# A recurrent chain with its router on one core: who halves the state, who selects, when GpSimd mixes, and how the first loads are cut

## What is computed

```python
def cell(h, x):
    gi = x @ W_ih + b_ih
    gh = h @ W_hh + b_hh
    i_r, i_z, i_n = jnp.split(gi, 3, axis=-1)
    h_r, h_z, h_n = jnp.split(gh, 3, axis=-1)
    r = jax.nn.sigmoid(i_r + h_r)
    z = jax.nn.sigmoid(i_z + h_z)
    n = jnp.tanh(i_n + r * h_n)
    h_new = (1.0 - z) * n + z * h
...
probs = softmax(xt @ w_router)                       # 128 experts
topk_p, topk_idx = top_k(probs, 4)
topk_w = topk_p / (sum(topk_p) + EPS)
basis = silu(xt @ w_gate) * (xt @ w_up)              # K = 8 bases of I = 128 columns
mixed = einsum('tek,tki->tei', mix[topk_idx], basis)
out = einsum('teh,te->th', mixed @ w_down, topk_w * expert_scale[topk_idx])
out = out + silu(xt @ shared_w_gate) * (xt @ shared_w_up) @ shared_w_down
return x + out
```

## Time and profile before

| | |
|---|---|
| median of 3 executions | 148.21 us (148.15 to 151.74) |
| the profiled execution, device time | 147.87 us |
| its span, first to last instruction | 146.0 us |
| TensorE matmul, busy | 136.3 us (93%) |
| TensorE weight load, busy | 98.0 us (67%) |
| VectorE, busy | 111.6 us (76%) |
| ScalarE, busy | 68.1 us (47%) |
| GpSimd, busy | 68.9 us (47%) |

### The profile page before, as it was taken

One profiled execution on the slowest core, in us unless ns is written; L12 is line 12 of the kernel. 1 busy time (PEld: TensorE's weight loads), 2 busy tenths in 40 slices (PEclk: granted clock), 3 DMA queues, 4 the chain that ended last, 5 costly groups with the idle time before them and its releaser, 6 DMA issues.

```text
span 146.0 us, 4048 instructions
## 1 busy us (share of the span) xinstructions
PE 136.3 (93%) x1494; PEld 98.0 (67%) x1494; DVE 111.6 (76%) x411; ACT 68.1 (47%) x222; POOL 68.9 (47%) x123
## 2 busy tenths in 40 slices
PE   7997999999679989999999999999999998899981
PEld 5565767766347658766876687668766875597881
DVE  2215588998967997898789878987898789949661
ACT  1204638565557345535553555255526541522830
POOL 2201115667754893466147614751475148566030
PEclk9999999999999999999999999999999999999999
DMA  3898970000000000010001000100010000000102
GB/s 97 270 369 288 343 235 5 7 0 2 0 0 4 0 0 4 4 36 4 0 0 40 0 0 0 43 0 0 7 36 0 4 7 31 0 0 0 36 4 72
DMA packets 5799, 7.12 MB, mean 49 GB/s; under 512 B 916, under 2 KB 4244, under 8 KB 5780
## 3 DMA queue, kind: packets, MB, share of 16 engines
q1 hardware_dynamic: 5472, 6.70, 13.7%
q10 hardware_dynamic: 308, 0.17, 0.4%
HBM read 5.81 MB, written 1.05 MB: 47 GB/s over the span
## 4 chain that ended last, share of the span: by engine, by line
PE 51%; DVE 34%; ACT 7%; issue 3%; POOL 1%; DVEq 0%
PE unit L604 18%; PE gates L595 11%; DVE sc_out L851 7%; PE down L674 6%; ACT sc_add L412 4%; DVE keys L934 4%; PE gates L559 4%; PE turned L744 3%; DVE pre L842 3%; DVE hT L858 3%; DVE m L839 2%; DVE p L899 2%; DVE wlo L871 2%; PE unit L574 2%; ACT trz L405 2%
## 5 line engine op out<-in xcount | busy, mean ns | idle before, releaser
L299 POOL CAST hThi<-hT 128x64 fp32r<-128x64 f32 x32 | 11.1, 347 | 54.5 <-DVE hT L858 54.1
L604 PE MATMUL unit<-whi,hThi 128*128 128x512 f32 x80 | 33.7, 421 | 2.7 <-POOL wlo L334 2.0
L604 PE MATMUL unit<-wlo,hThi 128*128 128x512 f32 x80 | 31.6, 395 | 0.0
L604 PE MATMUL unit<-whi,hTlo 128*128 128x512 f32 x80 | 31.6, 394 | 0.0
L405 ACT ACTIVATE trz<-gates 128x128 f32<-128x128 f32 x32 | 8.9, 277 | 43.8 <-PE gates L595 43.8
L595 PE MATMUL gates<-whh,hT 128*32 128x192 f32 x512 | 27.4, 332 | 1.7 <-DVE hT L858 1.1
L595 PEld LDWEIGHTS gates<-whh,hT 128*32 128x32 f32 x512 | 13.5, 109 | 12.7 <-DVE hT L858 5.6
L851 DVE TENSOR_TENSOR_SCAN sc_out<-sc_mul,sc_add 128x128 f32<-128x128 f32 x32 | 15.3, 479 | 8.0 <-ACT sc_add L412 7.7
L604 PEld LDWEIGHTS unit<-whi,hThi 128*128 128x128 f32 x80 | 15.1, 188 | 8.7 <-issue 3.5
L604 PEld LDWEIGHTS unit<-whi,hTlo 128*128 128x128 f32 x80 | 15.0, 188 | 3.5
L412 ACT ACTIVATE sc_add<-pre 128x64 f32<-128x64 f32 x32 | 10.3, 322 | 14.5 <-DVE pre L842 14.5
(11 more groups left out here) (129 smaller groups left out, 243.3 us busy)
## 6 DMA issues: line engine op xcount, KB each, us to landing
wraw<-in_L_ffn_w_gate_dram SPq DMA_DIRECT2D x2, 512.0 KB, 6.0
wraw<-in_L_ffn_w_up_dram SPq DMA_DIRECT2D x2, 512.0 KB, 7.8
out_dram<-ot SPq DMA_DIRECT2D x8, 128.0 KB, 2.0
xtok<-in_x_dram SPq DMA_DIRECT2D x7, 128.0 KB, 4.1
wih<-in_L_cond_W_ih_dram SPq DMA_DIRECT2D x2, 384.0 KB, 4.3
whh<-in_L_cond_W_hh_dram SPq DMA_DIRECT2D x1, 512.0 KB, 6.5
whh<-in_L_cond_W_hh_dram SPq DMA_DIRECT2D x1, 256.0 KB, 5.8
wraw<-L_ffn_shared_w_gate_dram SPq DMA_DIRECT2D x1, 256.0 KB, 7.5
```

The costliest lines, as they stand in the source:

```text
L299: pool.tensor_copy(hThi[:, c % 3, :, :, k], hT[:, c % 2, :, k, :]).then_inc(hThi_ready, 1)
L604: last = pe.matmul(dst, st[:, p % 3, s, :, :].rearrange("p b t -> p (b t)"), w[:, s, :, cols], start=(s == 0 and n == 0), stop=(s == KB - ...
```

## The change

- **VectorE to ScalarE:** halving the state (`halve`, after `prepare(t)` in ScalarE's queue), copying the logits, `negmax` and `keys`, and `den`. The router's low weights are now added in the same bank columns by matmuls of 128 columns, so a copy replaces the addition.
- **GpSimd:** the mixing of chunk p - 1 goes over four steps: `scale_basis` 0 and 1 as before, `half` one step later, `quarter` and `mixed` two steps later; `lo_down` goes from step 10 to step 12.
- **Units:** TensorE's slots k = 0 to 3 hold 6, 9, 6 and 9 unit matmuls instead of 9, 9, 6 and 6. `turn_hidden(p - 1)` goes from k = 2 to k = 3, between unit matmuls, and `project` from chunk p - 1 in k = 3 to chunk p - 2 in k = 2. The last router runs before the last unit of chunk 6.
- **Weights and x:** all splitting of weights is a step earlier; the first pair of x blocks is turned in step 0; the steps in `EARLY` are others, as many as before.
- **Start:** 10 warming matmuls instead of 16; h0 is loaded by four DMAs of 32 rows.

```diff
@@ -45,16 +45,16 @@
-WARM = 16
+WARM = 10
...
-EARLY = [4, 5, 6, 7, 10, 11, 14, 15, 18, 19, 22, 23, 26, 27, 30, 31]
+EARLY = [4, 5, 6, 7, 9, 10, 13, 14, 17, 18, 21, 22, 25, 26, 29, 30]
...
-TURN_PAIR = {1: 2, 2: 4, 3: 6}
-KEEP_PAIR_SCALAR = {1: 2}
+TURN_PAIR = {0: 2, 2: 4, 3: 6}
+KEEP_PAIR_SCALAR = {0: 2}
...
-HI_AT = [(0, 0), (0, 0), (0, 0), (0, 2), (2, 4), (4, 6), (6, 8), (8, 10)]
-LO_VECTOR_AT = [[], [], [], [], [2], [4], [5], [8]]
-LO_POOL_AT = [[], [], [], [0], [1], [3], [6], [7], [9]]
+HI_AT = [(0, 0), (0, 0), (0, 2), (2, 4), (4, 6), (6, 8), (8, 10)]
+LO_VECTOR_AT = [[], [], [], [2], [4], [5], [8]]
+LO_POOL_AT = [[], [], [0], [1], [3], [6], [7], [9]]
@@ -313,9 +317,11 @@
-            def add_basis(p):
+            def add_half(p):
...
+            def add_rest(p):
@@ -347,7 +353,10 @@
                 if p >= 1 and k == 0:
...
-                    add_basis(p - 1)
+                if p >= 1 and k == 1:
+                    add_half(p - 1)
+                if p >= 1 and k == 2:
+                    add_rest(p - 1)
@@ -356,13 +365,14 @@
-                    if t == TC + SKEW + 4:
+                    if t == TC + SKEW + 6:
...
-            add_basis(LAST - 1)
+            add_half(LAST - 1)
+            add_rest(LAST - 1)
@@ -376,7 +386,8 @@
         def _(act):
...
-            act.dma_start(h0[:, :], cond.rearrange("b (j c) -> j b c", j=NJ)).then_inc(ld_h0, 16)
+            for j in range(NJ):
+                act.dma_start(h0[Q * j:Q * (j + 1), :], cond[:, FJ * j:FJ * (j + 1)]).then_inc(ld_h0, 16)
...
             def keep_bias():
@@ -411,6 +422,11 @@
+            def halve(t):
+                act.wait_ge(h_ready, t + 1)
+                act.activation(natural(hhalf, slice(0, FJ)), by_block(sc_out, 1), ACT.Copy, scale=0.5)\
+                    .then_inc(hhalf_ready, 1)
             def hi_router():
@@ -433,8 +449,23 @@
+            def copy_logits(p):
+                act.wait_ge(logits_ready, p + 1)
+                if p >= 1:
+                    act.wait_ge(topk_step, TOPK_STEPS * p)
+                act.activation(lx[:, 0:E], route[:, LOGITS], ACT.Copy).then_inc(lx_ready, 1)
+            def topk_keys(p):
+                act.wait_ge(max_ready, p + 1)
+                act.activation(negmax[:, :], v8[:, 0:1], ACT.Copy, scale=-1.0).then_inc(keys_ready, 1)
+                act.activation(keys[:, 0:TOPK], v8[:, 0:TOPK], ACT.Copy).then_inc(keys_ready, 1)
+            def topk_den(p):
+                act.wait_ge(topk_step, TOPK_STEPS * p + 2)
+                act.activation(den[:, :], exsum[:, :], ACT.Identity, bias=sum4[:, :], scale=EPS).then_inc(den_ready, 1)
             def softmax_exp(p):
-                act.wait_ge(topk_step, TOPK_STEPS * p + 3)
+                act.wait_ge(keys_ready, 2 * p + 2)
@@ -480,21 +511,28 @@
                 if p < 0:
                     return
                 if k == 0:
+                    copy_logits(p)
                     if p >= 1:
                         tanh_gate(NU * p - 1)
+                    topk_keys(p)
                 elif k == 1:
                     softmax_exp(p)
                     tanh_gate(NU * p)
+                    topk_den(p)
                 elif k == 2:
                     tanh_gate(NU * p + 1)
-                    copy_emT(p)
+                    tanh_gate(NU * p + 2)
+                elif k == 3:
+                    if p == 0:
+                        hi_down()
+                    tanh_gate(NU * p + 3)
                     if p >= 1:
                         hi_turned(p - 1, turned, slice(0, 3), p)
-                elif k == 3:
-                    tanh_gate(NU * p + 2)
-                    tanh_gate(NU * p + 3)
-                    if p == 0:
-                        hi_down()
+
+            def early_slot(f):
+                p, k = f // TC, f % TC
+                if p >= 0 and k == 2:
+                    copy_emT(p)
             keep_bias()
             for c in range(NC):
@@ -502,14 +540,21 @@
+                    early_slot(t - TC - SKEW)
...
+                    if t < T - 1:
+                        halve(t)
...
+                early_slot(f)
...
+            copy_logits(LAST)
...
+            topk_keys(LAST)
...
+            topk_den(LAST)
@@ -613,37 +670,29 @@
-                    pe.matmul(route[:, LOGITS], hThi[:, p % 3, s, :, :].rearrange("p b t -> p (b t)"),
-                              wrouter[:, s, :, :].rearrange("p a e -> p (a e)"),
-                              start=(s == 0), stop=False, skip_group_check=True)
+                    for a in range(2):
+                        pe.matmul(route[:, LOGITS], hThi[:, p % 3, s, :, :].rearrange("p b t -> p (b t)"),
+                                  wrouter[:, s, a, :], start=(s == 0 and a == 0), stop=False, skip_group_check=True)
...
-                    last = pe.matmul(route[:, 0:E], hTlo[:, p % 3, s, :, :].rearrange("p b t -> p (b t)"),
+                    last = pe.matmul(route[:, LOGITS], hTlo[:, p % 3, s, :, :].rearrange("p b t -> p (b t)"),
...
             def unit(n, blocks):
...
-                if p == 0:
-                    for s in blocks:
-                        i = PIECES.index((u, s))
-                        if i in LO_VECTOR:
-                            pe.wait_ge(w_lo, LO_VECTOR.index(i) + 2)
-                        else:
-                            pe.wait_ge(w_lo_pool, LO_POOL.index(i) + 1)
...
-                last = three(unit_bank[n % NB][:, :].rearrange("p (g n) -> p g n", g=2), p,
-                             slice(UW * u, UW * (u + 1)), blocks)
+                last = three(unit_bank[n % NB][:, :].rearrange("p (g n) -> p g n", g=2), p, u, blocks)
...
             def turn_em(p):
-                pe.wait_ge(topk_step, TOPK_STEPS * p + 5)
+                pe.wait_ge(topk_step, TOPK_STEPS * p + 2)
...
             def coefficients(p):
@@ -723,21 +772,23 @@
                     if k == 0:
                         logits(p)
                         unit(NU * p, range(KB))
-                        unit(NU * p + 1, [0])
                     if k == 1:
-                        unit(NU * p + 1, [1])
-                        unit(NU * p + 2, range(KB))
+                        unit(NU * p + 1, range(KB))
+                        unit(NU * p + 2, [0])
                     if k == 2:
                         turn_em(p)
+                        unit(NU * p + 2, [1])
+                        unit(NU * p + 3, [0])
+                        if p >= 2:
+                            project(p - 2)
+                        coefficients(p)
+                    if k == 3:
+                        unit(NU * p + 3, [1])
                         if p >= 1:
                             turn_hidden(p - 1)
-                        unit(NU * p + 3, range(KB))
-                        coefficients(p)
-                    if k == 3:
-                        if p >= 1:
-                            project(p - 1)
+                        if p == LAST - 1:
+                            logits(LAST)
                         unit(NU * p + 4, range(KB))
-
             def keep_warm(count, dst=turned):
                 for _ in range(count):
@@ -772,10 +823,10 @@
-            logits(LAST)
...
+            project(LAST - 2)
@@ -856,7 +907,6 @@
                 if k == 0 and c >= 2:
...
-                dve.tensor_scalar(natural(hhalf, slice(0, FJ)), by_block(sc_out, 1), 0.5, None, ALU.mult).then_inc(hhalf_ready, 1)
             def lo_router():
@@ -919,42 +969,25 @@
-            def copy_logits(p):
-                dve.wait_ge(logits_ready, p + 1)
-                dve.tensor_reduce(lx[:, 0:E], route[:, LOGITS].rearrange("p (a e) -> p e a", a=2), mybir.AxisListType.X,
-                                  ALU.add).then_inc(lx_ready, 1)
             def topk_max(p):
...
-                dve.max(v8[:, :], lx[:, 0:E]).then_inc(topk_step, 1)
-            def topk_keys(p):
-                dve.wait_ge(topk_step, TOPK_STEPS * p + 1)
-                dve.tensor_scalar(negmax[:, :], v8[:, 0:1], -1.0, None, ALU.mult).then_inc(topk_step, 1)
-                dve.tensor_copy(keys[:, 0:TOPK], v8[:, 0:TOPK]).then_inc(topk_step, 1)
+                dve.max(v8[:, :], lx[:, 0:E]).then_inc(max_ready, 1)
             def topk_mark(p):
-                dve.wait_ge(topk_step, TOPK_STEPS * p + 3)
+                dve.wait_ge(keys_ready, 2 * p + 2)
...
             def topk_em(p):
-                dve.wait_ge(topk_step, TOPK_STEPS * p + 4)
+                dve.wait_ge(topk_step, TOPK_STEPS * p + 1)
...
-            def topk_den(p):
-                dve.wait_ge(topk_step, TOPK_STEPS * p + 5)
-                dve.scalar_tensor_tensor(out=den[:, :], in0=exsum[:, :], scalar=EPS, in1=sum4[:, :],
-                                         op0=ALU.mult, op1=ALU.add).then_inc(topk_step, 1)
-            def topk_rec(p):
-                dve.wait_ge(topk_step, TOPK_STEPS * p + 6)
-                dve.reciprocal(rec[:, :], den[:, :]).then_inc(topk_step, 1)
             def scale_coefficients(p):
```

(27 more changed lines are left out.)

25 lines of the change are left out of this document (20 added, 5 removed).

## The result

| | before | changed |
|---|---|---|
| all timed runs, median | 150.08 us (six runs, 148.15 to 151.98) | 152.61 us (six runs, 151.82 to 154.30) |
| ratio of comparable runs, 95% interval | 1 | 1.0289 (1.0260 to 1.0317) |
| the profiled execution | 147.87 us, span 146.0 | 153.46 us, span 151.7 |

The changed kernel is slower by 2.9%, where 149.8 us and no measurable change were forecast.

The account below looks back on a forecast made before the run. The prediction took TensorE's queue to bind most steps and VectorE one per chunk; 0.4 + 0.1 - 1.65 + 1.3 + 0.4 + 1.0 = +1.55 us gave 149.8 us, with a range of 147.7 to 151.6.

Parts of the forecast that it names:

- What bounds the kernel: Recurrent chunk: TensorE's queue binds steps k=0, 2, 3, VectorE k=1 through the `keys` copy; relief at most 0.23 us per chunk.
- Start, +0.4: Up to the first recurrent step: fewer warming matmuls, but TensorE waits for a later second x block; +0.4 us.
- second x block is late: Rival at the start: four issues take 0.69 each, first step 2.0 later instead of 0.4, 151.4 us; 15%.
- Steps 0 to 7, +0.1: First eight steps: x transposes and weight pieces move earlier, slots of steps 3 to 6 get shorter; sum +0.1 us.
- Steps 8 and 9, -1.65: First selection: waits for `wlo` vanish, step 8 takes 3.4 and step 9 3.07, 6.47 instead of 8.12 us.
- Steps 10 to 13, +1.3: `dlo_w` ahead of `quarter` and `mixed` makes TensorE stand 2.5 us in step 13; 16.3 against 14.98 us.
- T + 4.15: When GpSimd's `mixed` is ready, in us counted from T, the new state of step 12.
- Steps 14 to 30, +0.4: Later chunks: 14.52 against 14.45 us, VectorE's 0.23 eaten by the router's matmuls, 0.22; four chunks +0.3, step 30 3.67.
- the tail, +1.0: Step 31 to last unit matmul: one more `project` 1.08, router 0.2, three unit matmuls 0.7, less `keys` copy 0.97.
- rival of free matmuls: Rival in the router: six short matmuls cost no more than four, 8 x 0.22 less, 148.0 us; 17%.
- ScalarE's work at nothing: ScalarE's new small operations in step k=0 stay within the cover of 0.6 and 0.76 us, so cost nothing.
- The sum: Whole kernel: the terms add up to +1.55 us, 149.4 for the profiled execution, 149.8 for the median.

Follow-up runs that it names:

- b_keys_scalar: Kernel before, with `negmax` and `keys` made by ScalarE instead of VectorE; ratio 0.9981 (0.9950 to 1.0011).
- b_adds_cut: Kernel before, with GpSimd's additions `half`, `quarter`, `mixed` cut to 8 columns from the second chunk on; ratio 1.018.
- b_warm10: Kernel before, with 10 warming matmuls instead of 16; 150.53 us median of ten runs.
- b_both: Kernel before, with h0 in four DMAs and 10 warming matmuls; ratio 1.0103, 149.97 us median.
- a_x_ahead: Changed kernel, with the second x block issued ahead of the four DMAs of h0; ratio 1.0280.
- a_lodown_behind: Changed kernel, with `lo_down` behind `mixed` in the slot of step 12; ratio 1.0163, 150.42 us median.
- a_best: Changed kernel, with h0 in one DMA, 16 warming matmuls, `lo_down` behind `mixed`, router matmuls and VectorE's addition as before; ratio 0.9906.
- b_h0_four: Kernel before, with h0 in four DMAs of 32 rows; ratio 1.0222, 151.41 us median.
- a_h0_one: Changed kernel, with h0 loaded by one DMA again; ratio 1.0225 (1.0149 to 1.0300).
- a_warm16: Changed kernel, with 16 warming matmuls again and h0 still in four DMAs; 154.04 us median.
- a_best24: a_best with 24 warming matmuls instead of 16; 147.95 us median of twelve runs, ratio 0.9979.

## Why the prediction was wrong, point by point

- **What bounds the kernel: right about TensorE, wrong about why VectorE is late.** With VectorE relieved, a chunk is TensorE's in all four steps, 14.49 against 14.52 forecast. But the forecast took the `keys` copy's 0.97 for a cost that goes away with the copy. b_keys_scalar and b_adds_cut show it is a stand behind GpSimd. By b_adds_cut, what frees VectorE in step k=1 is GpSimd's additions going to other steps; the copy's move alone gains nothing measurable. What VectorE's other moved operations add was not run by itself.
- **Start, +0.4: the step that failed.** "I take 0.4, nearest the low bound": the four issues took 1.79 us together, 1.1 more than one, and nothing came back. The block, now issued behind both loads of whh (2.56 and 3.20), was there 2.1 later; that queueing behind them makes the other 1.0 is likely, but no run shows it. The rival *second x block is late* had +2.0 and 15%, and it came near the measured 2.27 for another reason than its own: the issues took 0.45 each, not 0.69. What neither had is the clock. "Six warming matmuls fewer let the bias matmuls start some 0.5 earlier" counts only their time; they are also what brings the clock up, and with ten it was late in eight of ten runs of b_warm10, by their times. By b_both the start costs some 1.5 us in timed runs.
- **Steps 0 to 7, +0.1, measured +0.4:** 26.72 to 27.45 in the variants of the changed kernel with the same first eight steps, against 26.96. Most of the difference within them is step 2, in which TensorE stopped for up to 0.7 in the middle of its matmuls; what stopped it is open.
- **Steps 8 and 9, -1.65, measured -1.0.** No wait for `wlo` is left, as forecast. But step 8 took 3.71, not 3.4, and step 9 3.42, not 3.07: VectorE holds both (0.06 from state to `h_part`), with `em` late behind ScalarE's `ex`, 0.54 for `mix` (beside GpSimd's `wlo`), and in step 9 `p`, `q`, `rec`, `coef` and `p` again ahead of the next gate. A floor of TensorE's was taken where the first selection binds. This is read from the trace alone; no variant tests it:

```profile
43.40 0.86 PE L640 MATMUL gates<-whh,hT 128*32 128x192 f32 x16 [0.25 <-DVE hT L909]
...
46.82 0.86 PE L640 MATMUL gates<-whh,hT 128*32 128x192 f32 x16 [0.27 <-DVE hT L909]
```

- **Steps 10 to 13, +1.3: mechanism and size right, one effect missing.** Forecast 16.3, with `mixed` ready at T + 4.15; measured 16.35 in three variants with the same queue and a steady clock, and T + 4.10 in the changed kernel's profile. On top comes the clock that falls behind the stall, 1.5 us in this profile and in that of a_x_ahead. In how many of the six timed runs it fell there is not known. Four have a mean clock of 0.986 or less, but a low clock at the start does that too (0.977 in a_lodown_behind, which has no stall), and two of the four took only 0.8 us more than the two whose mean clock was 0.994 and 1.0. The forecast said that "the whole recurrence stands" and did not ask what TensorE's clock does then.
- **Steps 14 to 30, +0.4, and the tail, +1.0: right in size** (+0.4, +0.8). In the tail this was luck in part: the 0.97 taken off for the copy of `keys` is the same misreading as above. With the copy alone moved (b_keys_scalar) the tail is 17.64, as before (17.62); what went in the changed kernel are three waits of TensorE for VectorE, 0.38, 0.41 and 0.27. The row's 0.11 for a short matmul held: in a_best two fewer gave back 0.21. The Trainium skill's 56 ns (TensorE: Matmul & The Clock Gate, "Wait — 56ns, not 53.3ns?") does not fit this stream, in which each of the two took 0.10, and the rival of free matmuls fell with it.
- **ScalarE's work at nothing: right.** 0.5 us or more remain from the state to the next `h_part` in all four steps of a chunk.
- **The sum.** Between the two profiles the span grew by 5.7 us where 1.55 was forecast. Of the 4.15 that were missing, the start is 1.9, the clock behind the stall 1.5, steps 8 and 9 0.7 and steps 0 to 7 0.3; the tail was 0.2 cheaper than forecast. For the timed runs the sizes are an estimate: start +1.5 (b_both), steps 8 and 9 -1.0, stall +1.4, chunks +0.4, tail +0.8, and +0.8 for what lowered the clock (the median of 152.6 less the 151.8 of the two runs without it), together +3.9 and 152.1 us; the median was 152.6, so 0.5 is not assigned. The range's upper end (151.6) had the late block but no clock.

## What to carry to other kernels

Price a stall or a start of TensorE twice: the idle time itself, and the matmuls at half pace behind it; so look where a moved operation lets TensorE stand, and keep `lo_down`-like work behind what TensorE waits for. A small operation with an absurd duration (four columns in 0.97 us) can be a wait in disguise: see what another engine runs beside it until the same moment, before giving the operation away. Cutting a small load into several is paid by whatever is issued behind it in the same queue (here 1.79 us of issues instead of 0.65).

## What was not expected of the hardware

- The start has more than one outcome with the same program. With 16 warming matmuls the bias matmuls took 1.04 us in one profile and 1.93 in another, and H(0) was 10.07 to 10.51 or 14.0 to 14.4 (12.85 in b_h0_four, where the wait for the block came between). In timed runs 24 warming matmuls gave no late start in 18 runs, 20 gave one in twelve, 16 in a_best three in six, and 10 on the kernel before eight in ten.
- Behind a wait of 2.4 us TensorE's clock fell in two profiles (the changed kernel's and a_x_ahead's, both at 61.5 us, 0.1 and 1.0 after the wait had ended) and stayed up in two (a_h0_one, a_warm16). In a wait of 4.67 it fell while TensorE stood. With 20 filling matmuls (2.36 us of them) the mean clock was 0.994 or more in all four runs. Why it falls in one run and not in another is open.
- VectorE's `sc_add` took 1.01 instead of 0.27 and the scan 0.93 instead of 0.42 beside GpSimd's additions, each ending 0.1 to 0.3 behind them.
- The pause of TensorE within step 2 (up to 1.3 us, in a_best24) is not explained. It appeared only in variants of the changed kernel, at 17 to 19 us from the start of the span.
